# Two attention blocks rebuilt: float32r operand parts, two row halves of the array, 1024-wide maxima

## What is computed

```python
scores = jnp.einsum('bqhd,bkhd->bhqk', q, k) / jnp.sqrt(jnp.float32(Dh))   # full, twice
attn = jax.nn.softmax(scores, axis=-1)
ctx = jnp.einsum('bhqk,bkhd->bqhd', attn, v).reshape(Bb, Ss, Dd)
x = x + ctx @ Wo
...
attn = jnp.where(causal[None, None], attn, -jnp.inf)                      # once, causal
attn = jax.nn.softmax(attn, axis=-1)
```

## Time and profile before

| | |
|---|---|
| median of 3 runs | 3383.09 us (3382.2 to 3384.76) |
| span of the profiled execution | 3382.5 us |
| PE, DVE, ACT, POOL busy | 3032.9, 2225.2, 1668.8, 168.7 us |
| heads of F, L, H (first score to last output copy) | 757, 571, 757 us |

### The profile page before, as it was taken

How to read it: one execution, slowest core, us unless ns; L and a number is a source line. 1 busy time by engine, 2 the same in 40 slices (tenths; PEclk the granted TensorE clock), 3 DMA queues, 4 the chain that set the end, 5 groups by cost and what they waited for, 6 DMA issues and landing times. The chain is left out here.

```text
span 3382.5 us, 48839 instructions
## 1 busy us (share of the span) xinstructions
PE 3032.9 (90%) x14997; PEld 1205.9 (36%) x14997; DVE 2225.2 (66%) x4191; ACT 1668.8 (49%) x2007; POOL 168.7 (5%) x88
## 2 busy tenths in 40 slices
PE   6788859999999997997799999958999999998998
PEld 2787732222222223443233333322222222222443
DVE  5444459988889893223667666647989888894322
ACT  4212123666666665433255555531666666666333
POOL 1222220000000000001100000011000000000000
PEclk9888866999999997998699999975999999999899
DMA  1000010110011011120111111111010000110211
GB/s 37 1 0 0 0 61 11 29 29 19 27 29 29 17 30 32 69 69 12 59 32 39 30 30 41 30 32 59 15 30 29 29 19 28 29 29 21 76 56 31
DMA packets 75059, 105.46 MB, mean 31 GB/s; under 512 B 17334, under 2 KB 48016, under 8 KB 72433
## 3 DMA queue, kind: packets, MB, share of 16 engines
q1 hardware_dynamic: 71755, 100.97, 9.8%
q10 hardware_dynamic: 3104, 1.94, 0.2%
HBM read 68.72 MB, written 20.55 MB: 26 GB/s over the span
## 5 line engine op out<-in xcount | busy, mean ns | idle before, releaser
L466 DVE TENSOR_REDUCE Hmaxes<-Hm 128x1 f32<-128x512 f32 x1044 | 658.2, 685 | 95.6 <-PE Hm L392 95.0
L466 DVE TENSOR_REDUCE Fmaxes<-Fm 128x1 f32<-128x512 f32 x1044 | 658.1, 685 | 95.5 <-PE Fm L392 95.1
L447 ACT ACTIVATE Hprob<-Hs 128x1024 f32<-128x1024 f32 x512 | 498.5, 1021 | 242.3 <-PE Hs L357 240.7
L447 ACT ACTIVATE Fprob<-Fs 128x1024 f32<-128x1024 f32 x512 | 498.5, 1021 | 242.1 <-PE Fs L357 240.6
L466 DVE TENSOR_REDUCE Lmaxes<-Lm 128x1 f32<-128x512 f32 (+3 forms) x664 | 373.1, 605 | 179.0 <-PE Lm L392 105.3
L447 ACT ACTIVATE Lprob<-Ls 128x1024 f32<-128x1024 f32 (+7 forms) x384 | 293.1, 776 | 268.5 <-PE Ls L360 144.8
L392 PE MATMUL Hm<-Hka,Hqa 99*128 99x512 bf16 x1044 | 381.6, 404 | 27.4 <-DMA Hvh<-Hvstack 11.5
L392 PE MATMUL Fm<-Fka,Fqa 99*128 99x512 bf16 x1044 | 381.4, 404 | 26.8 <-DMA Fvh<-Fvstack 11.0
L357 PE MATMUL Fs<-Fqa,Fka 99*128 99x512 bf16 x1024 | 308.3, 385 | 1.6 <-ACT Fprob L447 1.2
L357 PE MATMUL Hs<-Hqa,Hka 99*128 99x512 bf16 x1024 | 308.2, 384 | 1.6 <-ACT Hprob L447 1.2
L374 PE MATMUL Ho<-Hprob,Hvh 128*32 128x512 f32 x2048 | 276.3, 612 | 0.6 <-ACT Hprob L447 0.6
(11 more groups left out here) (428 smaller groups left out, 2883.7 us busy)
## 6 DMA issues: line engine op xcount, KB each, us to landing
FEwb<-FE_weights SPq DMA_DIRECT2D x8, 1024.0 KB, 5.9
HEwb<-HE_weights SPq DMA_DIRECT2D x8, 1024.0 KB, 5.3
Fqa<-F_qparts SPq DMA_DIRECT2D x51, 96.0 KB
Fka<-F_kparts SPq DMA_DIRECT2D x51, 96.0 KB
Lqa<-L_qparts SPq DMA_DIRECT2D x51, 96.0 KB
Lka<-L_kparts SPq DMA_DIRECT2D x51, 96.0 KB
Hqa<-H_qparts SPq DMA_DIRECT2D x51, 96.0 KB
Hka<-H_kparts SPq DMA_DIRECT2D x51, 96.0 KB
```

What stands on the lines that cost most here:

```text
L447: nc.scalar.activation(prob[:, kt % PSLOTS, q0:q1], sps[SLOT_OF[kt, half]][:, q0 - half * 1024:1024], ACT.Exp, scale=SCALE).then_inc(expd, 1)
L466: nc.vector.reduce_max(maxes[:, qt, kb:kb + 1], src[:, 0:n], AX.X).then_inc(max_free, 1)
```

## The change

- q and k are split into two float32r parts instead of three bfloat16 parts (one copy, one subtraction for each 512 tokens). All products of parts are 4 x 8 = 32 rows. A head's `qa` and `ka` hold them twice: on partitions 0 to 33 with the two rows for the maximum (scores), and on partitions 64 to 96 (maxima). Both matmuls use tiles of 64 rows and 128 columns, at row position 0 and 64.
- A maxima item is up to 1024 wide: two matmuls into a two-bank slot, two such slots, one reduction. A full head has 32 items, a causal head 24. Scores are in blocks of 512, in a ring of three one-bank slots, one exponential each; the transposes of maxima and of outputs pass through the same ring.
- TensorE's order for a key tile: the maxima matmuls are dealt out before each of its score blocks, then `weigh` of the key tile before.
- Causal: no mask matmuls. VectorE adds the mask while it reduces (a fused operation, 16 of 24 items), and GpSimd sets the upper triangle of `prob` to zero (`affine_select`) before `weigh`. `weigh` deals the queries out in interleaved groups of 128, so that its four column positions have equal widths.
- The split of the maxima and the placing of a head's values into `vh` move to GpSimd, the copy to `toprow` to ScalarE.
- Output: TensorE transposes `osb` (`deliver`), ScalarE writes numerators and sums token-major into `heads`, and one reciprocal and one product after the heads give the result; the way through DRAM goes. After F and H `project_tokens` transposes back and multiplies by Wo, after L `add_tokens` adds.
- v is projected at the start of the head block; fills of `qa`, `ka`, `vstack` shrink.

```diff
-PARTS = 3
-MROW = 96
+PARTS = 2
+MROW = PARTS * PARTS * DH
 KROWS = MROW + PARTS
-EARLY_FULL, EARLY_CAUSAL = 20, 24
+LOW = 64
+LROWS = MROW + 1
+EARLY_FULL, EARLY_CAUSAL = 8, 9
+TURN_FULL, TURN_CAUSAL = 13, 11
...
+            qa = sbo("qa", [P, 2, T], F32R)
...
+                    def maxima(h, i, s, j, n):
+                        qt, half, width = MAXES[j]
+                        if n == 0:
+                            if j == 0:
+                                pe.wait_ge(low_in[s], (i + 1) * LOADS)
+                            pe.wait_ge(max_free, h * NM + j + 1)
...
+                        last = nc.tensor.matmul(mps[j % 2][:, n * BANK:n * BANK + w],
+                                                qa[LOW:LOW + LROWS, s, qt * P:(qt + 1) * P],
+                                                ka[LOW:LOW + LROWS, s, k0:k0 + w], start=True, stop=True)
...
+                        pe.wait_ge(expd, entry(h, kt, n) + 1)
+                        nc.tensor.matmul(seat(kt, n)[:, 0:q1 - q0], ka[0:KROWS, s, kt * P:(kt + 1) * P],
+                                         qa[0:KROWS, s, q0:q1], start=True, stop=True).then_inc(scored, 1)
...
+                            for k in range(high):
+                                for ahead, j, n in low[round(len(low) * k / high):round(len(low) * (k + 1) / high)]:
+                                    maxima(h + ahead, i + (u + ahead) // 2, (u + ahead) % 2, j, n)
+                                score(h, i, u, kt, k)
+                            if kt > 0:
+                                weigh(h, u, kt - 1)
...
+                            nc.vector.tensor_tensor_reduce(
+                                out=mps[j % 2][:, 0:width], in0=mps[j % 2][:, 0:width], in1=later[:, 2 * BANK - width:2 * BANK],
+                                scale=1.0, scalar=LEAST, op0=ALU.add, op1=ALU.max,
+                                accum_out=maxes[:, qt, half:half + 1]).then_inc(max_free, 1)
...
+                                nc.gpsimd.affine_select(diag, diag, [[1, P]], ALU.is_ge, 0.0, base=0, channel_multiplier=-1)\
+                                    .then_inc(masked, 1)
...
+def add_tokens(nc, name, y, x):
...
+                nc.vector.tensor_tensor(x[:, :, :], x[:, :, :], y[:, :, :], ALU.add).then_inc(added, 1)
```

More of the change, by code:

```diff
@@ L6 @@
 F32 = mybir.dt.float32
-BF16 = mybir.dt.bfloat16
+F32R = mybir.dt.float32r
 ALU = mybir.AluOpType
@@ L212, in first_query, with blocks @@
+    ident = consts["ident"]
+    qscr = nc.dram_tensor(name + "_qparts", (PARTS, P, T), F32, kind="Internal").ap()
+    kscr = nc.dram_tensor(name + "_kparts", (PARTS, P, T), F32, kind="Internal").ap()
+    EARLY = EARLY_CAUSAL if causal else EARLY_FULL
+    TURN_AT = TURN_CAUSAL if causal else TURN_FULL
     def first_query(kt):
         return kt * P if causal else 0
-    def halves(kt):
-        return [h for h in range(2) if (h + 1) * 1024 > first_query(kt)]
-    def blocks(kt, half):
+    def blocks(kt):
@@ L219, in blocks @@
         lo = first_query(kt)
-        return [(max(lo, b * BANK), (b + 1) * BANK) for b in (2 * half, 2 * half + 1) if (b + 1) * BANK > lo]
-    MAXES = [(qt, kb, min(BANK, (qt + 1) * P - kb * BANK) if causal else BANK)
-             for qt in range(NT) for kb in range(NB) if not causal or kb * BANK <= qt * P]
-    NM = len(MAXES)
-    NHALF = sum(len(halves(kt)) for kt in range(NT))
-    SLOT_OF = {}
-    for kt in range(NT):
-        for half in halves(kt):
-            SLOT_OF[kt, half] = len(SLOT_OF) % 2
@@ L231, in attention @@
-    AHEAD = np.cumsum([0] + [len(halves(kt)) for kt in range(NT)]).tolist()
-    BEFORE = 1
-    EARLY = EARLY_CAUSAL if causal else EARLY_FULL
-    ITEMS = NM + 1
-    stream = ([(1, j) for j in range(EARLY, NM)] + [(2, j) for j in range(BEFORE)] + [(1, "turn")]
-              + [(2, j) for j in range(BEFORE, EARLY)])
-    def count(h, j):
-        if j == "turn":
-            return h * ITEMS + NM + BEFORE + 2
-        if j >= BEFORE:
-            return h * ITEMS + j + 2
-        return h * ITEMS + j + (2 if isinstance(h, int) and h == 0 else 1)
@@ L251, in attention, with keys @@
-    cost = lambda j: 250 if j == "turn" else 60 + MAXES[j][2]
-    done = np.cumsum([cost(j) for _, j in stream])
-    length = np.cumsum([T - first_query(kt) + STEP_COST for kt in range(NT)])
+        return [(q0, min(q0 + BANK, T)) for q0 in range(lo, T, BANK)]
+    def keys(qt):
+        return (qt + 1) * P if causal else T
+    MAXES = [(qt, half, min(2 * BANK, keys(qt) - 2 * BANK * half))
+             for qt in range(NT) for half in range(2) if keys(qt) > 2 * BANK * half]
+    NM = len(MAXES)
@@ new lines, in attention, with entry, out_entry, turn_entry @@
+    AHEAD = np.cumsum([0] + [len(blocks(kt)) for kt in range(NT)]).tolist()
+    NE = AHEAD[NT] + 2
+    BEFORE = NB + 1
+    OUT_AFTER = 1
+    def entry(h, kt, n=0):
+        return BEFORE + h * NE + AHEAD[kt] + n + (kt > OUT_AFTER) + (kt > TURN_AT)
+    def out_entry(h):
+        return BEFORE + h * NE + AHEAD[OUT_AFTER + 1]
+    def turn_entry(h):
+        return BEFORE + h * NE + AHEAD[TURN_AT + 1] + 1
+    def slot_of(offset):
+        return offset % 3
+    stream = [(1, j) for j in range(EARLY, NM)] + [(2, j) for j in range(EARLY)]
@@ L1536, in _ @@
                 nc.vector.tensor_copy(cols[:, :], cps[:, :]).then_inc(moved, 1)
[L1537 removed]
+                dve.wait_ge(moved, 2)
             @block.sync
```

753 lines of the change are left out of this document (386 added, 367 removed).

## The result

The changed kernel takes 3505.29 us (median of 5 executions, 3456.41 to 3687.49), the kernel before 3383.16: a ratio of 1.0295 [1.0237, 1.0354], slower, where I had forecast 3051. Executions of the changed kernel differ among themselves because the granted clock does (0.80 in the quickest, 0.72 in the slowest); the profiled one, on which all that follows rests, has a span of 3453.6 us.

The account below looks back on a forecast made before the run. The prediction took PE to bound the kernel in full and causal heads. From 3382.5 us it took 202 (full heads), 75 (causal heads) and 55 (ends), giving 3051 us; range for 8 in 10: 2960 to 3265.

Parts of the forecast that it names:

- The step that failed: Argument against a slower clock in the heads: PE never idle at the low level, and without gaps it returned to 0.99.
- clock rival: In the heads, PE waits for DVE and the clock falls to 1.2 GHz: 3835 us; some of it 0.09, 0.06 slower.
- Its point of decision: Low clock in some 40% of the heads' time decides the sign: a gain of 332 against a swing of 784.
- (a) one pass: Score and maxima matmuls: a float32r matmul takes one pass, 0.21 us, within bounds of 0.21 and 0.85.
- (b) pairs overlap: Two matmuls on different row halves overlap fully: 0.21 us a pair instead of 0.43.
- (c), the switch: Switching between row and column tiling in a key tile: no change, already within 0.13 and 0.15 us of frame.
- Full head 41.0: A full head (F, H) takes 41.0 us against 47.3, bounds 37 and 46.1; 32 heads give -202 us.
- I charge 0.2 us a key tile: Full heads: maxima waiting behind `weigh` add 0.2 us a key tile, 2.28 + 0.2 = 2.5.
- The bound moves from PE to DVE: Full heads: DVE at 37 us a head becomes the bound, with ACT beside it; PE needs about 32.5.
- My 2.28: Full heads: time of a key tile before the 0.2 us charged for the wait behind `weigh`.
- Causal head 31: A causal head takes 31 us against 35.7, bounds 25 and 33.8; 16 heads give -75 us.
- Ends -55: Outside the heads (projection, fills, first maxima, output ends): together -55 us, bounds -20 and -75.

Follow-up runs that it names:

- 64-row kernel: Changed kernel with scores and maxima contracting over 64 rows each instead of 34 and 33, the added rows zero: 3165.39 us, ratio 0.9367 to the kernel before.
- experiment 8: On the 64-row kernel, the previous key tile's output matmuls issued in the middle of a key tile instead of behind its last score: 3312.71 us, ratio 0.981.
- experiment 9: On the 64-row kernel, maxima 512 wide in three one-bank buffers and four score buffers instead of three: 3136.95 us, ratio 0.9292.
- experiment 7: On the 64-row kernel, VectorE reads only the first 512 columns of each 1024-wide maxima buffer: 3132.57 us, ratio 0.9248.
- experiment 13: On the 64-row kernel, 512-wide maxima and four score buffers in L, output matmuls of 14 key tiles a full head split in halves: 3052.33 us, ratio 0.9016.
- experiment 14: Changed kernel without added rows (33 and 34), with 512-wide maxima and four score buffers in the causal attention: 3408.96 us, ratio 1.0068.
- experiment 4: Changed kernel with the causal attention's code taken from the kernel before, F and H as changed: 3499.44 us (3333.39 to 3654.41), no ratio given.

## Why the prediction was wrong

The forecast misses the profiled execution by 3453.6 - 3050.5 = 403 us. The 64-row kernel divides that: 289 us are what its rows give back by the clock, and 114 are terms of the sum: 63 in the full heads, 40 in L (with what is left of the low clock there) and the rest outside the heads.

- **The step that failed**: "Against it: at the low level PE would be the bound and never idle, and in the full heads a PE without gaps came back to 0.99", on which the clock rival got 0.09. PE was nearly without gaps at the low level, as I said (71.00 us busy of 71.00 in F's first heads, 709 of 748 in the causal ones), and the causal heads stayed at 0.50 all the same. I took the clock as a matter of gaps. The runs showed that with the same instructions in the same order it follows the array rows over which the matmuls contract: 33 and 34 rows gave 0.50 in the causal heads, and 64, zeros or not, bring most of it back (0.91). How PE is fed counts beside the rows: at 64 rows the causal heads had 0.77 in experiment 8 and 1.00 in experiment 9. What the packing in row halves does to the clock by itself was not tried, since no run has short contractions one after the other. The two windows that I had (PE feeding VectorE alone, and the dip to 0.72) told of gaps because scores and maxima had the same 99 rows throughout. The Trainium skill (TensorE: Matmul & The Clock Gate, Part 1) also ties the gate to how busy PE is; the runs agree that work counts (experiments 8 and 9), but not that it is the whole rule (97% busy at 0.57 with 34 rows, 88% at 0.91 with 64).
- **The rival's own arithmetic** was near: key tile 3.7 us at 1.2 GHz, measured 4.08; causal head 42, measured 753/16 = 47.1. Its reason ("PE waits for DVE in every key tile") is not what the runs show. Its point of decision was "some 40% of the heads' time"; some 150 us of F, 75 of H and all 753 of L were spent at the low level, 44% of the heads' 2204 us, and the kernel was slower by 71. That this is so near is partly luck: gain and swing were both smaller than I had them (218 us with 64 rows instead of 332, and 289 us given back, where 44% of 784 are 345).
- **(a) one pass, (b) pairs overlap**: right. The first two pairs of a key tile start 0.00 to 0.01 us apart, and a float32r matmul takes 383 ns at the least, against 379 for the bfloat16 one of the earlier trace rows. But the second pair starts 0.34 us behind the first (903.01, 903.35), where the earlier trace rows has 0.23 (642.19, 642.42) and I had 0.21. This 0.1 us a key tile is missing in the 1.98 for PE. It stands behind the output matmuls, and a weight load of 0.19 us (0.10 in the trace of the kernel before) ends just ahead of it; whether it is that load or (c), the switch, was not tried. In the tile view of the changed kernel's `qa` (least, median and greatest ns, first and last start):

```profile
L271 PE MATMUL Fm<-Fka,Fqa x1024: 383/483/793, 491.6 to 1197.5; 33*128 33x512 f32 x171
...
L283 PE MATMUL Fs<-Fqa,Fka x1024: 383/493/792, 542.0 to 1274.9; 34*128 34x512 f32 x171
```

- **Full head 41.0**: 43.0 at the high level (688/16). "I charge 0.2 us a key tile" was 0.1 too low, and for the wrong reason: "The bound moves from PE to DVE" failed, although the signs that I had set for it came (VectorE busy 488 of 550 us, PE's waits mostly for `maxes`). VectorE's item is 1.18 us in a row, near my 1.14, but the chain is exponential, fourth score, output matmuls, first score, 2.62 us. Halving VectorE's work left it as it was (experiment 7), halving the output matmuls in it shortened F (experiment 13); that a fourth score buffer would have, no run shows. My 2.28 was the floor of an engine that doesn't decide.
- **Causal head 31**: 33.5 with 64 rows (536/16), where some stretches are still below 1.00, and 28.5 with four score buffers and narrow maxima. So how the banks are dealt out was worth 65 to 80 us in L (472 and 456 us against 536), part of it by the clock (0.91 and 1.00); my sum had no term for it. The Trainium skill (TensorEngine Tiling (Array Packing), Gotcha 1: PSUM Pressure) says that row tiling increases pressure on PSUM; here the banks went to wide maxima, and no run shows a price of the row tiling itself. The select, for which I had allowed 0.3 to 1.4 us, takes 0.295 and costs 11 us in all or nothing that can be told.
- **Ends -55**: -49 measured.

The rows by form of the changed kernel on which the select's price rests, and that of the fused maxima's second instruction (busy, mean ns):

```profile
L460 POOL TENSOR_SCALAR_AFFINE_SELECT Lprob<-Lprob 128x128 f32<-128x128 f32 x256 | 75.6, 295 | 672.4 <-ACT Lprob L408 672.4
```

```profile
L487 DVE DVE_READ_ACCUMULATOR2_ANT Lmaxes<- 128x1 f32 x256 | 36.2, 141 | 0.0
```

## What to carry over

Before matmuls are packed into row halves, ask how many rows of the array they still contract over; here contractions of 33 and 34 rows in the two halves ran at 1.2 GHz in a stage where 99 had held 0.97 of 2.4 GHz, and rows of zeros up to 64 cost nothing that could be measured but the fill. A clock that was high in the old kernel is no evidence for a new one with other shapes, even if PE never waits. And where engines pass work through a ring of buffers, write the chain down from one exponential to the next before summing the busy times: neither the engine with the largest sum nor the one that is waited for most need be in it.

## What I had not expected of the hardware

- At the same order of work the granted clock went with the rows (maxima/scores): causal heads 0.50, 0.56, 0.77 and 0.91 for 33/34, 48/48, 33/64 and 64/64. Why 64 for one kind does more than 48 for both is open, and so is whether the weight loads, which got the same rows, have a part in it.
- Full attentions of 33 and 34 rows leave the low level at very different times (some 75 us after the first score in F of the changed kernel, under 25 in F of experiment 14, 125 in H of experiment 4, over 190 in H of experiment 14), and executions of one binary differ by up to 10%. With 64 rows they agree to 0.4 to 1.3%.
- A loop body that grew made PE stand still for 3.5 us once in two heads in H, but not in F with the same code, and the instruction queue moved 106 packets instead of 50.
- VectorE's fused add and maximum is two instructions, of which the second takes 141 ns (mean of 256); I had allowed up to 0.28 us.
